# A graph transformer layer on one core: first expert weights behind the routing loop, residual tiles loaded in the expert stage, and a combining loop whose sums run one tile ahead

## The reference

```python
def _L0_ffn_ref(x, Wr, br, W1, b1, W2, b2, ln_g, ln_b):      # x is layernorm(x2), x2 the sum so far
    probs = softmax(einsum('bsd,de->bse', x, Wr) + br)
    top_vals, top_idx = top_k(probs, 2)                       # two of 8 experts for each token
    routing_weights = top_vals / sum(top_vals)
    h = gelu(einsum('bsd,edh->besh', x, W1) + b1)             # 768 -> 192, one W1 for each expert
    y = einsum('besh,eho->beso', h, W2) + b2                  # 192 -> 768
    out = einsum('beso,bse->bso', y, expert_weights)
    mu, var = mean(out), var(out)                             # over the 768 features
    return (out - mu) * rsqrt(var + 1e-5) * ln_g + ln_b
x = x2 + _L0_ffn_ref(layernorm(x2), ...)
```

## Time and profile before

| | us |
|---|---|
| runs before: median of 3 | 3599.15 (3598.68 to 3605.56) |
| the profiled execution, its own time | 3594.7 |
| its span, first to last instruction | 3592.9 |
| busy over the span: PE, DVE, POOL, ACT | 3106.6, 1944.3, 1503.7, 1125.4 |
| routing, start of its loads to the next stage's first load | 2999.4 to 3149.1 |
| experts | 3149.1 to 3445.4 |
| combining, first load to the end of the span | 3445.4 to 3592.9 |

### The profile page before, as it was taken

The page is one execution under the profiler, slowest core; times in us unless marked ns, Lnnn a source line. Parts: engine busy times, 40 slices in busy tenths (PEclk is TensorE's granted clock), DMA queues, the critical chain, the costliest instruction groups (busy, mean ns, idle before and its releaser), DMA issues. The chain is left out here.

```text
span 3592.9 us, 63295 instructions
## 1 busy us (share of the span) xinstructions
PE 3106.6 (86%) x21962; PEld 2542.8 (71%) x21963; DVE 1944.3 (54%) x4537; ACT 1125.4 (31%) x2419; POOL 1503.7 (42%) x1497
## 2 busy tenths in 40 slices
PE   7974999999999789999799995999999996589920
PEld 6973677777777568889799995666666663389920
DVE  4853667666666554444522222666666664633357
ACT  2322434343434243333412221333333322223321
POOL 1323677777777400000000002777777751233346
PEclk9997999999999899999899997899999996689965
DMA  5746788888888465544466674999999975456767
GB/s 184 235 160 198 238 264 261 269 259 264 264 268 263 129 202 139 136 136 140 171 82 86 87 88 150 352 325 327 326 326 328 327 269 192 156 198 239 237 229 255
DMA packets 275948, 786.79 MB, mean 219 GB/s; under 512 B 81326, under 2 KB 94353, under 8 KB 272438
## 3 DMA queue, kind: packets, MB, share of 16 engines
q0 software_dynamic: 96640, 416.68, 35.5%
q1 hardware_dynamic: 178998, 366.17, 34.6%
HBM read 676.48 MB, written 167.42 MB: 235 GB/s over the span
## 5 line engine op out<-in xcount | busy, mean ns | idle before, releaser
L940 POOL DMA_INDIRECT k_rows<-tab,k_pick x576 | 598.1, 1038 | 234.7 <-issue 175.1
L2161 POOL DMA_INDIRECT m_rows<-tab,m_e x500 | 490.0, 980 | 200.8 <-issue 143.4
L1400 PE MATMUL k_num<-k_rows,k_wt 128*32 128x384 f32 (+1 forms) x3200 | 283.2, 494 | 14.3 <-ACT k_wt L1032 14.3
L142 PE MATMUL g_prod<-g_w_hi,g_h_h 128*128 128x384 f32 x768 | 258.0, 336 | 3.4 <-DVE g_h_l L1766 3.4
L143 PE MATMUL g_prod<-g_w_lo,g_h_h 128*128 128x384 f32 x768 | 257.8, 336 | 0.0
L144 PE MATMUL g_prod<-g_w_hi,g_h_l 128*128 128x384 f32 x768 | 257.8, 336 | 0.0
L1661 PE MATMUL f_prod<-f_a_h,f_w_hi 128*128 128x512 f32 (+1 forms) x672 | 253.9, 378 | 2.5 <-DVE f_w_lo L1604 2.5
L1663 PE MATMUL f_prod<-f_a_h,f_w_lo 128*128 128x512 f32 (+1 forms) x672 | 246.5, 367 | 0.0
L1662 PE MATMUL f_prod<-f_a_l,f_w_hi 128*128 128x512 f32 (+1 forms) x672 | 246.4, 367 | 0.0
L1730 POOL MEMSET g_row<- 128x1 f32 x2 | 0.1, 101 | 542.3 <-issue 542.3
L1597 DVE TENSOR_TENSOR f_a_l<-f_turn,f_a_h 128x512 fp32r<-128x512 f32 (+1 forms) x168 | 98.8, 628 | 210.1 <-ACT f_a_h L1564 210.1
(11 more groups left out here) (366 smaller groups left out, 7675.5 us busy)
## 6 DMA issues: line engine op xcount, KB each, us to landing
agg<-k_outb SPq DMA_DIRECT2D x100, 384.0 KB
f_a_in<-agg SPq DMA_DIRECT2D x100, 384.0 KB, 7.3
g_h<-h SPq DMA_DIRECT2D x25, 1024.0 KB, 12.1
ys<-e_y SPq DMA_DIRECT2D x56, 384.0 KB, 2.9
h<-f_e SPq DMA_DIRECT2D x16, 1024.0 KB, 5.2
tab<-q_xn SPq DMA_DIRECT2D x25, 388.5 KB, 5.4
tab<-g_row SPq DMA_DIRECT2D x25, 385.5 KB, 4.6
m_own<-tab SPq DMA_DIRECT2D x25, 385.5 KB, 9.0
```

Source lines behind the costliest of these rows:

```text
L142: pe.matmul(out, x_hi[k], w_hi[k], start=(k == 0), stop=False)
L940: pool.indirect_dma_start(rows[:, place(u, n), :], None, dram["tab1"], at, bounds_check=bound, oob_is_err=False).then_inc(rows_in[i], 16)
L1400: mm = pe.matmul(num[i][o, 0:n], wt[u % 2][:, v, o], rows[:, place(u, 2 * (half + v) + g), a:a + n], start=(v == 0), stop=(v == 1), tile_p ...
L2161: pool.indirect_dma_start(rows[:, place(h, c) + k, :], None, tab, bass.IndirectOffsetOnAxis(ap=e[h % 4][:, 0, k * SLOTS + c:k * SLOTS + c ...
```

## The change

1. `phase_route`: the six loads of `w1` leave the tile loop and are issued by SP behind it.
2. `phase_experts`: with each of the last six stores of expert tiles SP also loads one residual tile (`xs` tiles 0 to 5) into six new buffers `rest`, which live over both stages (a new pool "z" around them).
3. `phase_combine`: the residual ring is these six buffers instead of four of its own. SP loads none at the start; from tile 2 on it loads tile `t + 4` ahead of the store of tile `t`. DVE's "both" of tile `t + 1` now stands between "gain" and "result" of tile `t`, and `y` has three buffers instead of two, so that ACT may write tile `t` once result `t - 3` is done. `layernorm_stats` waits for `gain_done` of the tile before.

```diff
-                if 8 <= t < 8 + KC:
-                    k = t - 8
-                    sp.dma_start(moe["w1"][:, k, :], io["eW1"][k * P:(k + 1) * P, :]).then_inc(w_in, 16)
+            for k in range(KC):
+                sp.dma_start(moe["w1"][:, k, :], io["eW1"][k * P:(k + 1) * P, :]).then_inc(w_in, 16)
...
                 sp.dma_start(dram["ys"][j * P:(j + 1) * P, :], y[j % YR][:, :]).then_inc(y_out[j % YR], 16)
+                t = j - (ETILES - REST)
+                if t >= 0:
+                    sp.wait_ge(xs_out[t % SR], 16 * (t // SR + 1))
+                    sp.dma_start(moe["rest"][t][:, :], dram["xs"][t * P:(t + 1) * P, :]).then_inc(moe["rest_in"][t], 16)
...
-            load_x(0)
             sp.dma_start(gain[:, :], io["ln_g"].partition_broadcast(P)).then_inc(c_in, 16)
-            load_x(1)
             for t in range(NT):
-                if t + 2 < NT:
-                    load_x(t + 2)
+                if t >= 2 and t + XR - 2 < NT:
+                    load_x(t + XR - 2)
                 store(t)
...
+            both(0)
+            for t in range(NT):
+                b = t % 3
+                dve.wait_ge(y_done, t + 1)
+                if t:
+                    dve.wait_ge(gain_done, t)
+                layernorm_stats(dve, y[b], st, mv, stats_done, stats_seen, mean_done, t)
...
                 dve.scalar_tensor_tensor(out=y[b][:, :], in0=y[b][:, :], scalar=mv[:, 0:1], in1=gain[:, :], op0=ALU.subtract,
                                          op1=ALU.mult).then_inc(gain_done, 1)
...
+                if t + 1 < NT:
+                    both(t + 1)
+                result(t)
...
-        phase_experts(nc, io, dram, keep, moe)
-        phase_combine(nc, io, dram, keep, moe, out)
+        with Pool(nc, "z") as z:
+            moe["rest"], moe["rest_in"] = [z.sb(f"rest{b}", [P, D]) for b in range(REST)], [z.sem(f"rest_in{b}") for b in range(REST)]
+            phase_experts(nc, io, dram, keep, moe)
+            phase_combine(nc, io, dram, keep, moe, out)
```

More of the change, by code:

```diff
@@ L46 @@
 HC = DHID // 2
+REST = 6
 ETILES = (2 * N + NEXP * (P - 1)) // P
@@ L3045, in phase_combine @@
     R = 4
+    XR = REST
+    x, x_in = moe["rest"], moe["rest_in"]
     with Pool(nc, "o") as s:
-        x = [s.sb(f"x{b}", [P, D]) for b in range(R)]
         g = [[s.sb(f"g{i}{b}", [P, D]) for b in range(R)] for i in range(2)]
-        y = s.sb2("y", [P, D])
+        y = [s.sb(f"y{b}", [P, D]) for b in range(3)]
         gain = s.sb("gain", [P, D])
         st, mv, vps, rstd = s.sb("st", [P, 2, 6]), s.sb("mv", [P, 2]), s.sb("vps", [P, 1]), s.sb("rstd", [P, 1])
-        c_in, x_in, stored = s.sem("c_in"), [s.sem(f"x_in{b}") for b in range(R)], [s.sem(f"stored{b}") for b in range(R)]
+        c_in, stored = s.sem("c_in"), [s.sem(f"stored{b}") for b in range(XR)]
         g_in = [[s.sem(f"g_in{i}{b}") for b in range(R)] for i in range(2)]
@@ L3061, in load_x @@
             def load_x(t):
-                if t >= R:
-                    sp.wait_ge(stored[t % R], 16 * (t // R))
-                sp.dma_start(x[t % R][:, :], dram["xs"][t * P:(t + 1) * P, :]).then_inc(x_in[t % R], 16)
+                sp.wait_ge(stored[t % XR], 16 * (t // XR))
+                sp.dma_start(x[t % XR][:, :], dram["xs"][t * P:(t + 1) * P, :]).then_inc(x_in[t % XR], 16)
             def store(t):
@@ L3068, in store @@
                 sp.wait_ge(sum_done, t + 1)
-                sp.dma_start(out[t * P:t * P + n, :], x[t % R][0:n, :]).then_inc(stored[t % R], 16)
-            load_x(0)
+                sp.dma_start(out[t * P:t * P + n, :], x[t % XR][0:n, :]).then_inc(stored[t % XR], 16)
             sp.dma_start(gain[:, :], io["ln_g"].partition_broadcast(P)).then_inc(c_in, 16)
-            load_x(1)
             for t in range(NT):
-                if t + 2 < NT:
-                    load_x(t + 2)
+                if t >= 2 and t + XR - 2 < NT:
+                    load_x(t + XR - 2)
                 store(t)
-            for b in range(R):
-                sp.wait_ge(stored[b], 16 * ((NT - b + R - 1) // R))
+            for b in range(XR):
+                sp.wait_ge(stored[b], 16 * ((NT - b + XR - 1) // XR))
         @blk.gpsimd
@@ L3101, in _, with both, result @@
                 act.wait_ge(g_in[0][t % R], 16 * (t // R + 1))
-                if t >= 2:
-                    act.wait_ge(sum_done, t - 1)
-                act.activation(y[t % 2][:, :], g[0][t % R][:, :], ACT.Copy, scale=moe["gate"][:, 0, t:t + 1]).then_inc(part_done, 1)
+                if t >= 3:
+                    act.wait_ge(sum_done, t - 2)
+                act.activation(y[t % 3][:, :], g[0][t % R][:, :], ACT.Copy, scale=moe["gate"][:, 0, t:t + 1]).then_inc(part_done, 1)
         @blk.vector
         def _(dve):
-            for t in range(NT):
-                b = t % 2
+            def both(t):
+                b = t % 3
                 dve.wait_ge(part_done, t + 1)
                 dve.wait_ge(g_in[1][t % R], 16 * (t // R + 1))
+                dve.scalar_tensor_tensor(out=y[b][:, :], in0=g[1][t % R][:, :], scalar=moe["gate"][:, 1, t:t + 1], in1=y[b][:, :],
+                                         op0=ALU.mult, op1=ALU.add).then_inc(y_done, 1)
+            def result(t):
+                b = t % 3
+                dve.wait_ge(gain_done, t + 1)
+                dve.wait_ge(rstd_done, t + 1)
+                dve.wait_ge(x_in[t % XR], 16 * (t // XR + 1))
+                dve.scalar_tensor_tensor(out=x[t % XR][:, :], in0=y[b][:, :], scalar=rstd[:, 0:1], in1=x[t % XR][:, :], op0=ALU.mult,
+                                         op1=ALU.add).then_inc(sum_done, 1)
+            both(0)
+            for t in range(NT):
+                b = t % 3
+                dve.wait_ge(y_done, t + 1)
+                if t:
+                    dve.wait_ge(gain_done, t)
+                layernorm_stats(dve, y[b], st, mv, stats_done, stats_seen, mean_done, t)
                 if t == 0:
                     dve.wait_ge(c_in, 16)
[L3114 to L3117, removed]
                 dve.wait_ge(mean_done, t + 1)
```

5 lines of the change are left out of this document (removed).

## The result

| | us |
|---|---|
| changed kernel, median of 4 runs | 3576.18 (3571.55 to 3578.54) |
| kernel before, median of 4 runs | 3600.30 (3598.68 to 3605.56) |
| ratio | 0.9929 (95% interval 0.9912 to 0.9946) |
| profiled execution, its own time and span | 3578.49, 3576.7 |

The profiled execution is at the upper end of its runs, and its routing starts 2.9 us later than in the profile before, for which no part of the change stands. From there to the end it took 574.4 us against 593.5, 19.1 less. The kernels were measured again later: over two profiles of the kernel before and three of the changed one this length is 23.4 us less on the mean, which agrees with the medians.

A forecast was written before the change was run, and what follows sets the result against it. Bounds: transfers in routing's loop while `w1` loads, PE in experts, DVE in combining with DMA close behind. 10.8 + 2.3 + 10.1 - 1.4 = 21.8 us less, median 3599.15 to 3577.4, range 3566 to 3588.

The forecast's parts named there:

- Routing, 10.8 us: Routing loop: without the `w1` loads, tiles 8 to 16 go at 3.64 us instead of 4.99, 10.8 us less.
- upper end of 13: Routing: the most that moving `w1` was taken to gain, 13 us; the lower end was 5.6.
- Six loads in the expert stage at no cost: Expert stage: six residual loads beside a DMA share of 0.25 cost 0, or 1 us if the last store is delayed.
- The start: Start of combining: with fewer loads queued, the first sum follows the second gather by 5.6 us, not 7.9; 2.3 less.
- Barriers, 1.4 us: Semaphore clearing: two more barriers with a clear, at 0.7 us each, 1.4 us more; ends 1 and 2.
- Combining's loop, 10.1 us: Combining: 19 periods of 4.75 us and 5 of 4.5 make 112.8 against 122.9, 10.1 us less.
- Case A: Combining tile: `vps` is held through gain and `rstd` through both, so result waits; period 4.88 us.
- case B: Combining tile: `rstd` gets in at gain's end and result starts right behind both; period 4.33 us.
- 11 of A and 14 of B: Combining: split of 25 tiles read from 15.8 us of waiting for `rstd`; gives a mean period of 4.57 us.
- first rival: Combining: `rstd` held in every tile, 4.88 us each, loop gains 5.8, total 3581.7 us; chance 0.20.
- rule on the shared port: Combining: VectorE and GpSimd share a port, first starter keeps it; taken strictly, gain starts first and every tile is Case A.
- Slower than before: Rival in combining: late gathers hold back finished results; landings decide from 9.0 us, at 9.9 total is 3609; chance 0.04.

The follow-up runs named there:

- experiment with tiles 17 to 22: Kernel before, with the six `w1` loads in routing tiles 17 to 22 instead of 8 to 13; 3588.69 us, ratio 0.9982.
- kernel with the memset: Changed kernel plus one 128x1 memset on VectorE between mean and gain in each combining tile; ratio 0.9927 to the kernel before, loop 114.6 us.
- last version: Changed kernel plus the memset, with gathers issued one tile earlier; 3559.13 us, ratio 0.9894 to the kernel before, when run again.
- kernel with `w1` alone: Kernel before, with only the six `w1` loads moved behind the routing loop; ratio 0.9962, routing 133.2 us.

## Why the prediction was right, and where it was not

- **Routing, 10.8 us.** Right, and a little small: 10.5 in the first pair of profiles, 12.7 between the means. The pace of tiles 4 to 8 was the right one to carry over (3.3 to 3.6 us a tile in the nine profiles, forecast 3.64). The upper end of 13 was passed twice, by routings of 133.2 and 135.7 us, and the first even passes the 14.2 us that I had called "more than any gain can be": it stands 16.5 below the mean. A rate of 332 GB/s was not the most that the transfers reach, as the experiment with tiles 17 to 22 shows (346).
- **Six loads in the expert stage at no cost.** Right: experts took 292.9 us before and after, to their last store. The start gained 3.3 us, not 2.3, as the first sum came 4.6 us after the second gather and I had taken the middle of loaded landings, 5.6.
- **Barriers, 1.4 us.** 0.54 at the end of the experts and 0.5 at the end of the program, 1.0 in all. SP's waits grew by only 0.6 us for the two additional steps (1.8 for 1.2), so 0.6 each was too much to carry over.
- **Combining's loop, 10.1 us.** 6.5 in the first pair of profiles, 9.4 between the means (129.6 and 120.2). From the first mean to the last it took 116.4, 114.6 and 114.6 us in the three profiles of the changed kernel, where I had 112.8. Case A was worked out right in each of its terms (forecast 4.88, measured 4.86 to 4.87), case B too (4.33; measured 4.21 to 4.22 in the kernel with the memset, where result takes 1.00 us and not 1.08). But how the total came together failed in two steps that nearly cancelled, and that is luck. "A tile moves two gathers, one residual load and one store: 0.92 x 5.12 = 4.71 us of all 16 engines" made transfers the bound. They are not: the last version moves the same in 4.22 us, at share 0.99 and 369 GB/s. And "11 of A and 14 of B" was the draw of one profile. The same program had 21 of A the next time, and the changed one has 21 or 22. It was luck again that the kernel before, profiled another time, took 2.4 us more in its loop than in the profile I had: that is a good part of the way from 6.5 to 9.4. So the first rival, `rstd` held in nearly every tile, is what took place, with a few late gathers; the measured 4.78 to 4.85 lies between its price of 4.88 and my 4.70.
- **The rule on the shared port** (Trainium skill, SBUF — State Buffer, "SBUF: two separate sides"). On who is held and for how long, the traces agree: 1.01 us for 0.18. That whichever starts first keeps the port can't be read off the starts: in the kernel before gain's start is recorded 0.05 us ahead of `vps` in all 25 tiles, the 11 held ones and the 14 free ones. Gain's own duration does tell them apart, with 1.02 us in the held tiles and 1.04 in the free ones, in the kernel before and, wherever gain starts first, in the changed one. A free tile of the changed kernel, beside the held one above:

```profile
3500.43 1.04 DVE L3135 SCALAR_TENSOR_TENSOR o_y<-o_y,o_mv,o_gain 128x768 f32<-128x768 f32 x1
3500.48 0.18 POOL L194 TENSOR_TENSOR o_vps<-o_mv,keep_ln_eps 128x1 f32<-128x1 f32 x1 [0.16 <-DVE o_mv L188]
```

  With the memset, which puts some 0.06 us more ahead of gain's reads, `vps` is never held. That fits a race which `vps` now wins, but no record shows the race itself.
- **Slower than before.** Late gathers did hold back results, but no gather of the changed kernel took over 8.0 us to land in the two of its three profiles that show landings, under the 9.0 from which it would have decided, and their waits lay where `rstd` was waited for anyway.

What stays open: why executions with the old order had 11, 13, 20 or 21 held tiles; and why the routing of the kernel with `w1` alone was 133.2 us when the other eight took 135.7 to 140.2 (its tiles 8 to 16 are like theirs, 26.9 us for 26.6 to 28.8; 1.8 us of it lie in the chain behind the loop).

## What to carry to other kernels

Putting an independent VectorE operation over a wait for GpSimd hides only part of the wait when that operation holds GpSimd too: here the period of a held tile fell from 5.25 to 4.86 us, that of a free one from 5.01 to 4.22. Look whether the small GpSimd operation's duration in the trace ends with a VectorE instruction, and if it does, try to give it a moment without reads ahead of the long instruction. A DMA share near 0.92 is no bound to divide by: compare GB/s with the most that another stretch of the same trace moves, and take even that for less than the limit (332 in the trace before, 369 in the last version). Where two waits can cover each other, take away both before judging either.

## What the runs showed of the hardware that was not expected

- A 128x1 memset of 0.06 us on VectorE ahead of a long two-input operation took nothing off VectorE's pace and let GpSimd in: `vps` 0.18 to 0.19 us instead of 1.01 in 25 of 25 tiles, period 4.21 instead of 4.86.
- The DMA share rose from 0.91 to 0.99 while the rate rose from 301 to 369 GB/s, so the share is not a measure of work done; the median landing of a gather was 6.7 us at both.
- On two of the chips the stages ahead of routing took 3416 to 3486 us for 2993 to 3002, while the three stages behind them took the same time as elsewhere, combining with `vps` on DVE at 363 GB/s among them. What slows the stages ahead is not shown.
